# Attention of a macaron block on one Trainium2 core: from pairs of batch and head to 64 units of 128 queries

## The reference

```
x = x + 0.5 * ffn(layernorm(x))          # x: 2 batches, 512 tokens, 512 columns
x = x + attention(layernorm(x))
x = x + 0.5 * ffn(layernorm(x))

ffn:        a = h @ (gate_w * (gate_su @ gate_sv)).T,  b = the same with up;  d = silu(a) * b
            out = d @ (down_w * (down_su @ down_sv)).T          # 1792 inner columns
attention:  q = h @ Wq.T (32 heads of 128),  k, v = h @ Wk.T, h @ Wv.T (8 heads of 128)
            q = rmsnorm(q) * q_norm_w,  k = rmsnorm(k) * k_norm_w
            scores = q k / sqrt(128) + slope_of_head * (key - query), causal
            out = softmax(scores) v, of all heads, @ Wo.T       # 4 query heads share one k and v head
```

## Time and profile before

| | us |
|---|---|
| median of 3 runs | 1401.33 (1400.23 to 1402.26) |
| the profiled execution | 1401.79 |
| its span, first to last instruction | 1400.5 |
| first feed-forward part, until the first `project` | about 272 |
| attention, until the last `project_out` | about 882 (272 to 1154) |
| rest | about 246 |

### The profile page before, as it was taken

One profiled execution on the slowest core, in us unless ns is written; L12 is line 12 of the kernel. 1 busy time (PEld: TensorE's weight loads), 2 busy tenths in 40 slices (PEclk: granted clock), 3 DMA queues, 4 the chain that ended last, 5 costly groups with the idle time before them and its releaser, 6 DMA issues.

```text
span 1400.5 us, 19159 instructions
## 1 busy us (share of the span) xinstructions
PE 1329.0 (95%) x7052; PEld 1129.8 (81%) x7052; DVE 959.1 (68%) x2263; ACT 587.2 (42%) x1436; POOL 361.9 (26%) x302
## 2 busy tenths in 40 slices
PE   5999999989999999999999999999999989999999
PEld 4888888777888878888878878888788768888887
DVE  6444444869779779779778778878888984444444
ACT  4222223246346446436436536545545633222221
POOL 4222223423023023123123222221321301222220
PEclk9999999999999999999999999999999999999999
DMA  5011111001001001001001001001001010111111
GB/s 205 0 48 48 49 48 48 30 6 66 6 1 46 31 1 46 31 1 46 31 1 46 31 0 46 31 1 46 30 1 49 1 48 1 48 48 49 48 48 60
DMA packets 13004, 49.92 MB, mean 36 GB/s; under 512 B 2064, under 2 KB 3408, under 8 KB 10864
## 3 DMA queue, kind: packets, MB, share of 16 engines
q1 hardware_dynamic: 12912, 48.70, 9.8%
HBM read 46.60 MB, written 2.10 MB: 35 GB/s over the span
## 4 chain that ended last, share of the span: by engine, by line
PE 79%; DVE 14%; ACT 5%; issue 1%; SPq 0%; DMA 0%; DVEq 0%
PE bank L176 24%; PE bank L177 24%; PE bank L178 24%; PE bank L302 4%; DVE prob L743 3%; ACT prob L485 3%; PE bank L279 2%; ACT probT_h L492 1%; DVE root_a L599 1%; DVE prob L731 1%; DVE probT_l L751 1%; DVE root_b L601 1%; DVE x_rows L768 1%; PE bank L191 1%; PE bank L200 1%
## 5 line engine op out<-in xcount | busy, mean ns | idle before, releaser
L865 POOL TENSOR_TENSOR w_l_late<-raw_late,w_h_late 128x512 fp32r<-128x512 f32 (+1 forms) x74 | 113.2, 1551 | 281.8 <-ACT w_h_late L446 141.0
L654 DVE TENSOR_TENSOR d<-bank,silu 128x512 f32<-128x512 f32 x56 | 38.7, 691 | 203.9 <-PE bank L178 203.9
L176 PE MATMUL bank<-w_h_late,xnT_hi 128*128 128x512 f32 (+1 forms) x512 | 176.0, 344 | 0.2 <-DVE top L731 0.2
L178 PE MATMUL bank<-w_h_late,xnT_lo 128*128 128x512 f32 (+1 forms) x512 | 173.7, 339 | 0.0
L177 PE MATMUL bank<-w_l_late,xnT_hi 128*128 128x512 f32 (+1 forms) x512 | 173.3, 339 | 0.0
L485 ACT ACTIVATE prob<-prob,neg_top 128x128 f32<-128x128 f32 (+3 forms) x256 | 140.9, 565 | 4.4 <-DVE neg_top L734 4.4
L892 POOL TENSOR_TENSOR row_room<-row_room,root_y 128x512 f32<-128x512 f32 x64 | 66.3, 1068 | 234.2 <-DVE root_y L603 234.2
L492 ACT CAST probT_h<-bank 128x512 fp32r<-128x512 f32 (+1 forms) x192 | 86.5, 522 | 91.8 <-PE bank L302 91.7
L743 DVE TENSOR_SCALAR prob<-prob,inverse 128x128 f32<-128x128 f32 (+3 forms) x256 | 118.3, 525 | 2.3
L176 PE MATMUL bank<-o_h,oT_h 128*128 128x512 f32 x256 | 107.5, 420 | 11.0 <-DVE oT_l L757 7.0
L731 DVE CUSTOM_DVE_ANT_0 prob<-bank,bias 128x128 f32<-128x128 f32 (+3 forms) x256 | 110.4, 485 | 1.0
(11 more groups left out here) (112 smaller groups left out, 3370.5 us busy)
## 6 DMA issues: line engine op xcount, KB each, us to landing
raw_late<-w_qkv SPq DMA_DIRECT2D x8, 1536.0 KB, 6.7
raw_early<-ffn_w SPq DMA_DIRECT2D x21, 512.0 KB, 4.9
raw_late<-ffn_w SPq DMA_DIRECT2D x21, 512.0 KB, 4.5
raw_late<-w_o SPq DMA_DIRECT2D x8, 1024.0 KB, 4.8
x_rows<-x SPq DMA_DIRECT2D x8, 256.0 KB, 4.6
y<-x_rows SPq DMA_DIRECT2D x8, 256.0 KB, 2.0
fac_raw_gu<-ffn_fac SPq DMA_DIRECT2D x28, 32.0 KB, 3.3
fac_raw_down<-ffn_fac SPq DMA_DIRECT2D x14, 32.0 KB, 4.5
```

The lines of the kernel that those rows point to most:

```text
L176: pe.matmul(bank, lh, rh, start=first, stop=False)
L178: return pe.matmul(bank, ll, rh, start=False, stop=last)
L865: return pool.tensor_tensor(lo, raw, hi.bitcast(F32), ALU.subtract)
```

## The change

Attention is cut into 64 units (`UNITS`): a unit is 128 queries of one batch with the four heads of one group. A slot of each engine's program works on unit n, on the rest of unit n-1, and projects unit n+4 (`LEAD`).

- `scores`: four heads, each with (i+1)·128 keys for the i-th block of queries. `turn_probabilities`: block j of all four heads in one bank, i+1 banks of 512 columns. `weigh_values`: i+1 blocks, each with 512 moving columns (v is still the weights).
- `project_out` adds the four heads up in one bank, so a token block of a group has one result.
- The scaling of the probabilities moves from DVE to ACT (`probabilities`), four instructions a unit. The maximum is taken negated (`ALU.min` with a factor -(2^-g)), so negating it and halving the bias on POOL fall away. q_scale of a group holds both norm weights, 1/sqrt(128) and 2^g.
- Squares of q and k move from DVE to POOL (`square_rows`), and POOL scales q and k together (`norm_rows`): two instructions of 640 columns a unit. DVE sums the squares and does the chain of roots for two units at a time (`pair_roots`, 32 of them instead of 16, in one piece).
- The split qkv weights lie in a ring of six chunks (`CHUNKS`), two of the next group's chunks are split in slot 2 of a group and two in slot 3. PE waits for the weights chunk by chunk.
- At the end, the roots and rows of the layer norm are spread over the last slots, half of the first `gate_up` stands in front of the last `turn_probabilities`, and `weigh_values` and `project_out` of the last unit stand between parts of the first step of the second feed-forward part. The rows of `normalize` share one buffer of four blocks for both batches.

The excerpt goes through the programs of PE, ACT, DVE and POOL in this order; the loop over `group` is gone in all of them.

```diff
+UNITS = HKV * B * TB
+LEAD = 4
+CHUNKS = KC + 2
+AHEAD = CHUNKS - KC
...
+            def turn_probabilities(n):
+                for j in range(unit(n)[2] + 1):
+                    r, bank = result("turn_prob", n, j)
+                    for h in range(G):
+                        if j == 0:
+                            pe.wait_ge(prob_done, n * G + h + 1)
+                        last = pe.transpose(bank[:, h * P:(h + 1) * P], prob[:, h, j * P:(j + 1) * P], ident[:, :])
+                    last.then_inc(full[r.bank], 1)
+            def weigh_values(n):
+                _, b, i = unit(n)
+                values = results["kv", n]
+                pe.wait_ge(evac[values.bank], values.nth)
+                r, bank = result("values", n)
+                for j in range(i + 1):
+                    turned = results["turn_prob", n, j]
+                    pe.wait_ge(evac[turned.bank], turned.nth)
+                    last = matmul3(bank[:, :], (v_h[:, b, j, :], v_l[:, b, j, :]),
+                                   (probT_h[:, j, :, :].rearrange("p h q -> p (h q)"), probT_l[:, j, :, :].rearrange("p h q -> p (h q)")),
+                                   j == 0, j == i)
+            def project_out(n):
+                g = unit(n)[0]
+                weighed = results["values", n]
+                pe.wait_ge(evac[weighed.bank], weighed.nth)
+                r, bank = result("out", n)
+                for h in range(G):
+                    if n % (B * TB) == 0:
+                        pe.wait_ge(o_lo, g * G + h + 1)
+                    last = matmul3(bank[:, :], (oT_h[:, h, :], oT_l[:, h, :]), (o_h[:, h, :], o_l[:, h, :]), h == 0, h == G - 1)
...
+            def slot(n):
+                scores(n)
+                if n:
+                    weigh_values(n - 1)
+                if n + LEAD < UNITS:
+                    project(n + LEAD, "q")
+                if n + 1 < UNITS:
+                    turn_rows(n + 1)
+                if n + LEAD < UNITS:
+                    project(n + LEAD, "kv")
+                elif n < UNITS - 1:
+                    scale_weights(1, 0, KINDS[n + LEAD - UNITS])
+                if n:
+                    project_out(n - 1)
+                if n == UNITS - 1:
                     turn_normed(2, 0)
+                    gate_up(1, 0, 0, 0, (0,))
+                turn_probabilities(n)
...
+            for n in range(UNITS):
+                slot(n)
+            gate_up(1, 0, 0, 0, (1,))
+            weigh_values(UNITS - 1)
+            gate_up(1, 0, 1, 0)
+            project_out(UNITS - 1)
+            down(1, 0, 0)
+            gate_up(1, 0, 0, 1)
+            scale_weights(1, 1, "gu0")
...
+            def probabilities(n):
+                keys = (unit(n)[2] + 1) * P
+                act.wait_ge(inverse_done, n + 1)
+                for h in range(G):
+                    p = prob[:, h, 0:keys]
+                    act.activation(p, p, ACT.Copy, scale=inverse[:, h:h + 1]).then_inc(prob_done, 1)
...
+            def slot(n):
+                g, at = divmod(n, B * TB)
+                exponentials(n)
+                if n:
+                    weigh_values(n - 1)
+                probabilities(n)
+                if at == 1:
+                    split_o(g, (2, 3))
+                if n + LEAD < UNITS:
+                    project_q(n + LEAD)
+                if n + 1 < UNITS:
+                    turn_rows(n + 1)
+                if n + LEAD < UNITS:
+                    project_kv(n + LEAD)
+                elif n < UNITS - 1:
+                    scale_weights(1, 0, KINDS[n + LEAD - UNITS])
+                if g < HKV - 1 and at == LEAD - 2:
+                    split_qkv(g + 1, range(AHEAD))
+                if g < HKV - 1 and at == LEAD - 1:
+                    split_qkv(g + 1, range(AHEAD, KC))
...
+                if at == 0:
+                    split_o(g, (0, 1))
...
+            def sum_squares(n):
+                dve.wait_ge(squares_done, n + 1)
+                dve.tensor_reduce(sums[:, n % 2, :], square[:, n % 2, :, :], AX.X, ALU.add).then_inc(sums_done, 1)
+            def pair_roots(n):
+                dve.wait_ge(sums_done, n + 2)
+                dve.wait_ge(rows_normed, n)
+                for last in inverse_root(row_roots, sums[:, :, :].rearrange("p u h -> p (u h)"), RMS_EPS, slice(0, ROOTS), 1.0 / HD):
+                    pass
                 last.then_inc(root_done, 1)
...
+            def scores(n):
+                g, _, i = unit(n)
+                keys = (i + 1) * P
+                for h in range(G):
+                    r = results["scores", n, h]
                     dve.wait_ge(full[r.bank], r.nth)
+                    dve.tensor_tensor_reduce(prob[:, h, 0:keys], banks[r.bank][:, 0:keys], bias[:, h, S - keys:S],
+                                             -(2.0 ** -g), -MASKED, ALU.add, ALU.min, neg_top[:, h:h + 1]).then_inc(evac[r.bank], 1)
+            def invert_sums(n):
+                dve.wait_ge(exp_done, n + 1)
+                dve.reciprocal(inverse[:, :], total[:, :]).then_inc(inverse_done, 1)
...
+            def slot(n):
+                scores(n)
+                if n + LEAD - 1 < UNITS:
+                    sum_squares(n + LEAD - 1)
+                invert_sums(n)
+                if n:
+                    weigh_values(n - 1)
+                if n % 2 == 0 and n + LEAD - 2 < UNITS:
+                    pair_roots(n + LEAD - 2)
+                if n == UNITS - 2:
                     normalize(2, 0)
+                if n + 1 < UNITS:
+                    turn_rows(n + 1)
+                if n == UNITS - 3:
+                    normal_roots(0)
+                if n + LEAD < UNITS:
+                    values_lo(n + LEAD)
+                elif n < UNITS - 1:
+                    scale_weights(1, 0, KINDS[n + LEAD - UNITS])
+                if n:
+                    project_out(n - 1)
+                if n == UNITS - 1:
+                    normal_roots(1, range(TB - 1))
                     turn_normed(2, 0)
+                turn_probabilities(n)
...
+            def square_rows(n):
+                pool.wait_ge(rows_copied, n + 1)
+                if n >= 2:
+                    pool.wait_ge(sums_done, n - 1)
+                row = rows[:, n % LEAD, :, :]
+                pool.tensor_tensor(square[:, n % 2, :, :], row, row, ALU.mult).then_inc(squares_done, 1)
+            def norm_rows(n):
+                pool.wait_ge(root_done, n // 2 + 1)
+                row = rows[:, n % LEAD, :, :]
+                by = row_root[:, n % 2, :].unsqueeze(2).to_broadcast([P, G + 1, HD])
+                pool.tensor_tensor(row, row, by, ALU.mult).then_inc(rows_normed, 1)
+            def slot(n):
+                g, at = divmod(n, B * TB)
+                if at == 1:
+                    split_o(g, range(G))
+                if n + 2 < UNITS:
+                    norm_rows(n + 2)
+                if n + LEAD < UNITS:
+                    square_rows(n + LEAD)
+                elif n < UNITS - 1:
+                    scale_weights(1, 0, KINDS[n + LEAD - UNITS])
+                if g < HKV - 1 and at == LEAD - 2:
+                    split_qkv(g + 1, range(AHEAD))
+                if g < HKV - 1 and at == LEAD - 1:
+                    split_qkv(g + 1, range(AHEAD, KC))
```

More of the change, by code:

```diff
@@ L28 @@
 STEPS = FI // P // CH
-PAIRS = B * G
 KINDS = ("gu0", "gu1", "down")
@@ L199, in turn_normed, with gate_up @@
                     for k in range(KC):
[L200 removed]
+                        last = pe.transpose(bank[:, k * P:(k + 1) * P], xn[:, t, k * P:(k + 1) * P], ident[:, :])
                     last.then_inc(full[r.bank], 1)
[L203 removed]
+            def gate_up(p, s, c, b, halves=(0, 1)):
                 kind = KINDS[c]
@@ new lines, in project @@
+            def project(n, part):
+                g, b, t = unit(n)
+                cols = slice(0, QW) if part == "q" else slice(QW, QKVW)
+                if g == 0:
+                    turned = results["xn", 1, b, t]
+                    pe.wait_ge(evac[turned.bank], turned.nth)
+                tokens = slice(b * S + t * P, b * S + (t + 1) * P)
+                r, bank = result(part, n)
+                for k in range(KC):
+                    if n % (B * TB) == 0:
+                        pe.wait_ge(qkv_lo, g * KC + k + 1)
+                    at = (g * KC + k) % CHUNKS
+                    last = matmul3(bank[:, 0:cols.stop - cols.start], (xnT_hi[:, k, tokens], xnT_lo[:, k, tokens]),
+                                   (qkv_h[at][:, cols], qkv_l[at][:, cols]), k == 0, k == KC - 1)
+                last.then_inc(full[r.bank], 1)
@@ L464, in norm_k, with project_q @@
-            def norm_k(g, b):
-                act.wait_ge(root_done, row_nth(g, b) + 1)
-                for t in range(TB):
-                    last = act.activation(rows[:, b, t, G, :], rows[:, b, t, G, :], ACT.Copy, scale=root[:, t, G:G + 1])
-                last.then_inc(k_normed, 1)
-            def turn_k(g, b):
-                r = results["turn_k", g, b]
```

(38 more changed lines are left out.)

632 lines of the change are left out of this document (214 added, 418 removed).

## The result

| | median us (lowest to highest) | profiled execution | span |
| --- | --- | --- | --- |
| before | 1401.62 (1400.23 to 1402.26) | 1401.8 | 1400.5 |
| after | 1330.3 (1329.37 to 1330.56) | 1330.4 | 1329.1 |

The ratio is 0.9491, 95% interval 0.9475 to 0.9508: 71 us faster. The forecast was 1349 (1328 to 1382), 19 us too slow but with the time inside the range, 2 us above its lower end.

A forecast was written before the change was run, and what follows sets the result against it. PE was taken to bound the kernel. From the profiled 1401.8 us, seven groups at 6.8 us less (47.6) and the start (4.5) came off, the end 0: 1349.7, with the median 0.5 lower 1349 us; range 1328 to 1382.

The forecast's parts named there:

- Own work of PE: Attention group: PE's matmuls and transposes summed from start to start, 98.5 us after the change against 99.6 before.
- What was kept beside it: Attention group: 1.2, 0.7 and 0.7 us on top of PE's 98.5, giving 101.1 us a group.
- small losses: Attention group: restarts behind a wait and small waits for a bank, 1.2 us of 2.0 kept (bounds 0.8 and 2.0).
- the switch: Attention units: first matmul behind transposes takes 0.32 instead of 0.234 us, at two places a unit; 0.7 us more a group.
- The wait for w_o: Every group: PE waits for the lo part of w_o, rests done on POOL; 0.7 us (bounds 0 and 4.8).
- The waits for DVE: Attention group: five PE waits, 5.4 us before; for the probabilities, q and k put at 0 (bounds 0 and 1).
- Rival E: Attention groups: w_o's rests all on the path, 8 x 4.1 = 33 us more, 1382; chance 0.07.
- B: Attention: ACT's order sets the slot, scalings ahead of copies PE awaits; 0.5 us a unit, 32 us, 1381; chance 0.13.
- C: Attention: 32 chains of roots held beside POOL, 3.2 us each, less 1 us cover; 72 us more, 1421; chance 0.04.
- D: Less left: no w_o wait, 0.8 not 1.2, no switch cost, end 6 us better; 20 us less, 1329; chance 0.15.
- Start: Start of attention: 5.5 us saved before the first scores, less about 1 in two slots; 4.5 us (bounds 2 and 6).
- End: End of attention: old wait of 5.11 us gone, less cover and chains of roots against it; 0, bounds 6 either way.

The follow-up runs named there:

- The run with four additions: Kernel after, with four unused POOL additions of 640 columns in every second unit, when DVE forms the rows' roots: 1359.8 us, ratio 0.9704.

## Why the prediction was right, and where it was off

**Own work of PE: right, some 0.5 us high.** 98.5 us were worked out for a group; the period is 98.6. The sum takes 0.234 us for every matmul of 512 columns; in the projections of the kernel after, twelve take 2.75 us, so 0.229.

**What was kept beside it: wrong, and the largest miss.** The forecast kept 1.2 us of small losses, 0.7 for the switch from transposes to matmuls and 0.7 for w_o, and got 101.1. The period is only 0.1 above the own work as summed, or some 0.6 with the pitch just named. The 2.0 us that the earlier trace rows left over in a clean group went with the rewrite. What they were is not shown: with the largest wait alone gone (the run with one wait more on POOL), 104.2 - 99.6 - 2.8 = 1.8 us of them were still there.

The switch was counted twice. PE at one of the 16 places of a group, and its weight load for a later matmul, in the kernel after:

```profile
393.20 0.60 PE L300 MATMUL bank<-ident,prob 128*128 128x128 f32 x4
393.56 0.36 PE L178 MATMUL bank<-kT_h,qT_h 128*128 128x256 f32 x1
393.76 0.29 PE L179 MATMUL bank<-kT_l,qT_h 128*128 128x256 f32 x1
...
395.27 0.19 PEld L178 LDWEIGHTS bank<-probT_h,v_h 128*128 128x128 f32 x1 [0.24 <-issue]
```

The first matmul behind the transposes does take 0.20 instead of 0.12 us, as in the earlier trace rows. But it starts that much earlier: four transposes and one matmul take 0.56 us, which is 4 x 0.109 + 0.12, and the sum of PE's own work had that already. The last row is a loss that is left, 0.24 us twice a group: it says "issue", but PE needs probT_l of the shortest unit there, which DVE finishes at 395.15. Seven groups of 2.5 us are 17.4 us, and with the average of all six periods of before, 108.1 us and not 107.9, it is 18.7.

**The wait for w_o: right in kind, 0.6 us too large.** The rests on POOL, and the weight load and the matmuls of the fourth head, in a slot that starts at 393.56, in the kernel after:

```profile
400.27 2.55 POOL L812 TENSOR_TENSOR o_l<-raw_late,o_h 128x512 fp32r<-128x512 f32 x2 [2.70 <-ACT o_h L441]
```

```profile
402.88 0.19 PEld L178 LDWEIGHTS bank<-o_h,oT_h 128*128 128x128 f32 x1 [0.23 <-POOL o_l L812]
...
402.92 0.46 PE L178 MATMUL bank<-o_h,oT_h 128*128 128x512 f32 x1
403.22 0.39 PE L179 MATMUL bank<-o_l,oT_h 128*128 128x512 f32 x1
```

PE asks for it with the weight load, at 402.88 - 0.23 = 402.65, 9.1 us into the slot where the forecast had 9.0. POOL ends at 402.82, 9.3 us into it where the forecast had 9.7. So POOL does come last, by 0.2 us. PE was still at work on the matmuls before, and only 0.07 us arrive at the matmuls (403.22 - 402.92 = 0.30 instead of 0.23), where the forecast had 0.7. Rival E (all four rests on the path) is out.

**The waits for DVE: right.** None is left (5.4 us a group), and the dips of the clock went with them (0.9). DVE is busy for 61 us of a group, as forecast; ACT for 66 instead of 72, POOL for 32 instead of 35. The scalings on ACT took 0.554 us on average against 0.565 assumed. The Trainium skill (ScalarE: Activation LUTs, Rules for kernel authors) would have left them on VectorE. Its ground is borne out (0.48 against 0.71 us for 512 columns), its verdict here is not: with them back on DVE the kernel is 3 us slower, all of it at the end.

**Rivals.** B needed ACT as the bound: the view has no wait for ACT in a group. C needed held root steps: 0.17 us each, because POOL has nothing to do at that moment. The run with four additions shows that C's mechanism is real and its price was too high: a chain held 4.4 us longer costs PE 0.7 us, since the cover is 3.7 us and not 1. D (less left than kept, 1329) is what happened in the groups, by the terms it named and 0.7 us a group beyond them; its end, 6 us better, did not come. That the time is nearly D's is luck: the loss at the end and the gain in the feed-forward parts, neither of them forecast, are 8 us each and cancel.

**Start: 4.5 us expected, 5.2 measured.** From the first projection to the first scores 298.31 - 272.18 = 26.1 us became 288.42 - 268.22 = 20.2, 5.9 less where 5.5 were worked out. From there to the first load 15.1 us became 15.8, 0.7 lost where the forecast took off 1; the row at 272.18 is that of the kernel before:

```profile
272.18 0.39 PE L176 MATMUL bank<-w_h_late,xnT_hi 128*128 128x512 f32 x1
```

**End: 0 expected, about 8 lost.** From the last load on, 9.5 us of a gapless period and 4 of the feed-forward part (see below) could have been saved, and 5.4 were. The prediction listed the causes (no projections as cover, chains of roots ahead of what PE awaits) and put them at nothing by setting the old waits against them. The largest was 4.7 us and a dip behind one chain, and moving that chain gave back 4 to 6 us.

**Not foreseen: 8 us in the feed-forward parts**, whose code the change does not touch. In sum, span against span with the forecast: groups 18.7, start 0.7 and feed-forward 7.9 better, end 8.0 worse, 19.3 together.

## What to carry to other kernels

A gap that stands between "own work" and "period" in a kernel with waits need not stay when the waits go: here 2.0 us became some 0.6 at most, though one wait alone took only 0.2 of it along. Where the own work is summed from start to start, a slower first matmul is in the sum already. Before an order is rewritten, look in the timeline for the one instruction of one engine that takes three times its usual duration beside another engine's; a single wait there may bring a third of the gain. Where buffers are added or resized, compare the start-to-start time of the same matmul before and after, also in stages that were not touched.

## What the runs showed of the hardware

- A matmul of 512 columns in gate_up took 0.2275 or 0.2333 us with the same code, by the distance of the weights to the normed rows in SBUF (256 bytes modulo 512 against 224, 320 and 384; `down` with a distance of 0 took 0.2275). That is 2.5% of gate_up, 8 us of this kernel. In the projections, with the two operands' parts exchanged, 320 was as fast as 256.
- The granted clock fell to half behind a wait of 4.7 us, with some 6 us at 1.2 GHz after it, and stayed at 2.4 GHz behind one of 2.2 us in the same place. Behind one of 2.1 us, 20 us earlier, it fell for over 3 us in the same kernel, and behind the wait of 2.5 us of the kernel before it fell in some groups (periods of 108.5 us) and not in others (107.0).
- Beside back-to-back additions of POOL (1.6 us each) DVE got one instruction through between two of them: its smallest steps (128x10) took 1.4 and 0.17 us in turn.
